# Every fourth unit's input product moves to GpSimd, fed by DMA, and x is fetched batch by batch

## What is computed

```
xp = xn @ w_xproj
dt_in, Bs, Cs = xp[..., :64], xp[..., 64:128], xp[..., 128:]
delta = softplus(dt_in @ w_dt + b_dt)
A = -exp(A_log)                                  # 128 channels x 64 states
h = exp(dt[:, :, None] * A) * h + (dt * xt)[:, :, None] * bt[:, None, :]
y = einsum('bdn,bn->bd', h, ct)                  # at each of 512 tokens
```

## Time and profile before

| | |
|---|---|
| median of 3 runs | 1300.27 us (1299.22 to 1301.88) |
| the profiled execution's own time | 1303.48 us |
| its span, first to last instruction | 1301.3 us |
| DVE busy | 1159.7 us, 89% of the span |
| POOL busy | 810.6 us, 62% |
| ACT busy | 777.0 us, 60% |
| PE busy | 931.7 us, 72% |
| DMA traffic | 155.29 MB, mean 119 GB/s |

### The profile page before, as it was taken

How to read it: one execution, slowest core, us unless ns; L and a number is a source line. 1 busy time by engine, 2 the same in 40 slices (tenths; PEclk the granted TensorE clock), 3 DMA queues, 4 the chain that set the end, 5 groups by cost and what they waited for, 6 DMA issues and landing times. The chain is left out here.

```text
span 1301.3 us, 19507 instructions
## 1 busy us (share of the span) xinstructions
PE 931.7 (72%) x4212; PEld 372.8 (29%) x4212; DVE 1159.7 (89%) x2546; ACT 777.0 (60%) x2103; POOL 810.6 (62%) x509
## 2 busy tenths in 40 slices
PE   4177767786777767777686867767768776867766
PEld 1022222322323222332233322232223322323222
DVE  4389999899898998979899798989999899997993
ACT  3168755586655864657556675457655586555761
POOL 6357766577564765658566675557756576665662
PEclk9559879689796877979778796878878787786977
DMA  4744457342673445534454335734267344663430
GB/s 104 126 113 122 110 123 174 98 130 79 138 171 95 131 110 135 137 91 131 115 136 132 105 98 124 171 101 120 79 144 174 94 133 110 136 157 100 120 98 8
DMA packets 124118, 155.29 MB, mean 119 GB/s; under 512 B 32719, under 2 KB 57056, under 8 KB 124000
## 3 DMA queue, kind: packets, MB, share of 16 engines
q1 hardware_dynamic: 123488, 153.73, 46.4%
q0 software_dynamic: 512, 0.27, 0.3%
HBM read 137.62 MB, written 4.52 MB: 109 GB/s over the span
## 5 line engine op out<-in xcount | busy, mean ns | idle before, releaser
L1381 POOL TENSOR_TENSOR prod<-hst,C 128x1024 f32<-128x1024 f32 x256 | 603.8, 2359 | 436.6 <-DVE hst L1177 431.1
L1177 DVE TENSOR_TENSOR_SCAN hst<-bank,dbx 128x512 f32<-128x512 f32 x512 | 617.5, 1207 | 8.6 <-ACT bank L645 8.4
L645 ACT ACTIVATE bank<-wide,A_rep 128x512 f32<-128x512 f32 x512 | 351.5, 687 | 407.7 <-DVE hst L1177 332.5
L1171 DVE TENSOR_TENSOR dbx<-bank,B 128x512 f32<-128x512 f32 x512 | 342.5, 669 | 77.6 <-PE bank L877 69.8
L877 PE MATMUL bank<-spread,sel_bc 96*128 96x512 bf16 x512 | 220.3, 445 | 118.2 <-DVE dbx L1171 98.9
L659 ACT ACTIVATE prob<-s_sb,nmax 128x96 f32<-128x96 f32 x512 | 183.8, 360 | 0.0
L911 PE MATMUL bank<-prod,sel_red 128*32 128x512 f32 x1024 | 176.5, 769 | 1.5 <-POOL prod L1381 1.5
L921 PE MATMUL bank<-k,q 128*128 128x384 f32 x256 | 137.7, 626 | 42.4 <-DVE nmax L1190 30.7
L877 PEld LDWEIGHTS bank<-spread,sel_bc 96*128 96x128 bf16 x512 | 54.3, 108 | 289.5 <-DVE dbx L1171 239.8
L928 PE MATMUL bank<-ident,prob 128*96 128x128 f32 x512 | 96.2, 321 | 42.5 <-ACT ao L675 42.5
L1386 POOL TENSOR_TENSOR prob<-prob,pinv 128x384 f32<-128x384 f32 x128 | 110.5, 863 | 10.8 <-DVE pinv L1198 7.9
(11 more groups left out here) (175 smaller groups left out, 949.7 us busy)
## 6 DMA issues: line engine op xcount, KB each, us to landing
wide<-rows SPq DMA_DIRECT2D x512, 256.0 KB, 4.4
vw<-v_tok SPq DMA_DIRECT2D x80, 64.0 KB, 3.3
spread<-parts SPq DMA_DIRECT2D x96, 32.0 KB, 1.9
x_sb<-in_L_attn_x_dram SPq DMA_DIRECT2D x8, 256.0 KB, 4.2
rows<-sp_t SPq DMA_DIRECT2D x8, 256.0 KB, 4.3
out_dram<-outb SPq DMA_DIRECT2D x8, 256.0 KB, 4.1
q<-qn SPq DMA_DIRECT2D x112, 16.0 KB
vw<-v_tok SPq DMA_DIRECT2D x16, 48.0 KB, 3.2
```

Source lines behind the costliest of these rows:

```text
L645: nc.scalar.activation(dtP[s % 2][:, :], steps, ACT.Exp, scale=A_rep[:, g:g + 1]) \
L1171: v.tensor_tensor(dbx[:, s % 3, :], steps, B2[p][:, :], ALU.mult).then_inc(dbx_done, 1)
L1177: v.tensor_tensor_scan(hst[:, s % 4, :], dtP[s % 2][:, :], dbx[:, s % 3, :], 0.0, ALU.mult, ALU.add).then_inc(scan_done, 1)
L1381: g.tensor_tensor(prod[:, 2 * (m % 4):2 * (m % 4) + 2, :], hst[:, 2 * (m % 2):2 * (m % 2) + 2, :], C2[p][:, :].unsqueeze(1).to_broadcast([ ...
```

## The change

The product u*B of every unit with q = 3 (16 of the 64 of a batch) is no longer formed by PE and DVE. The u rows of its channels, 96 to 127, are stored to DRAM (`u_rows`), read back by `widen_u` (two DMAs of 256 KB for two units, 16 DMAs a batch, a ring of 2 slots), and multiplied by B on POOL (`pool_input`, a TENSOR_TENSOR of 128x512 from SBUF into `gbx`), in slots 1, 5, 9, ... behind the pair product of that slot. `spread_parts` issues 9 DMAs where it issued 12.

x is no longer kept whole. SP loads batch B + 1 into `x_ln` at the beginning of body B, and once more batch B into `x_res` at m = 10 for the residual. `ln_stats` moves from slot 0 to 3, `ln_aggr` from 2 to 5, the five root steps from slots 4 to 8 to slots 6 to 10; `ln_apply` stays in slot 11. A wait of ACT for the stored rows before `k` is dropped.

The diff, cut to its core:

```diff
-    "ln_stats": 0, "ln_aggr": 2, "ln_root": 4, "ln_apply": 11, "scale_xn": 12, "softplus_exp": 23, "sum": 26,
+    "ln_stats": 3, "ln_aggr": 5, "ln_root": 6, "ln_apply": 11, "scale_xn": 12, "softplus_exp": 23, "sum": 26,
...
+U_SLOTS = 2
+POOL_Q = 3
+PE_Q = 3
+N_PARTS_DMA = 9
...
-            for b in range(1, NB):
-                x_load(b)
...
+                sp.dma_start(dt_rows[p], dtv[:, :]).then_inc(rows_out, 16)
+                sp.dma_start(u_rows[p], uv[32 * POOL_Q:32 * POOL_Q + 32, :]).then_inc(urows_out, 16)
...
+            def widen_u(B, p, m):
+                wait(sp, gbx_done, B * GROUPS + 2 * (m - U_SLOTS) + 2)
+                if m == 0:
+                    wait(sp, urows_out, (B + 1) * 16)
+                flat = u_rows.rearrange("a d t -> (a d t)")
+                for j in range(2):
+                    row = p * 32 + 4 * m + j
+                    src = bass.AP(flat.tensor, flat.offset + row * L, [[0, 64], [2 * L, 2], [1, L]])
+                    sp.dma_start(uwide[m % U_SLOTS][64 * j:64 * j + 64, :, :], src).then_inc(uwide_in[m % U_SLOTS], 16)
...
             def body(B, p):
+                if not last(B):
+                    wait(sp, ln_step, (B - 1) * N_LN + LN["xa"])
+                    x_load(B + 1, x_ln[1 - p], x_in)
                 for m in range(UNIT_PAIRS):
                     if m + SLOTS < UNIT_PAIRS:
                         widen(B, p, m + SLOTS)
                     elif not last(B):
                         widen(B + 1, 1 - p, m + SLOTS - UNIT_PAIRS)
+                    if m % 4 == 3:
+                        if m // 4 + U_SLOTS < GROUPS // 2:
+                            widen_u(B, p, m // 4 + U_SLOTS)
+                        elif not last(B):
+                            widen_u(B + 1, 1 - p, m // 4 + U_SLOTS - GROUPS // 2)
                     if m == ROWS_AT["store"] and not first(B):
                         store(B - 1, 1 - p)
+                    if m == ROWS_AT["store"]:
+                        x_load(B, x_res, xres_in)
...
+                if q == POOL_Q:
+                    return
...
             def unit_scan(B, s):
                 wait(dve, exp_done, B * UNITS + s + 1)
+                i, q = divmod(s, 4)
+                n = PE_Q * i + q
+                if q == POOL_Q:
+                    wait(dve, gbx_done, B * GROUPS + i + 1)
+                    into = gbx[:, i % 2, :]
+                else:
+                    wait(dve, dbx_done, B * PE_Q * GROUPS + n + 1)
+                    into = dbx[:, n % 3, :]
...
+            def pool_input(B, p, i):
+                if i == 0:
+                    wait(pool, done["p"], job_count("p", B, "B"))
+                if i % 2 == 0:
+                    wait(pool, uwide_in[(i // 2) % U_SLOTS], (B * (GROUPS // 2 // U_SLOTS) + i // 2 // U_SLOTS + 1) * 32)
+                wait(pool, scan_done, B * UNITS + 4 * i - 4)
+                g.tensor_tensor(gbx[:, i % 2, :], uwide[(i // 2) % U_SLOTS][:, i % 2, :], B2[p][:, :], ALU.mult) \
+                    .then_inc(gbx_done, 1)
...
                     if s % 2 == 1:
                         pair_product(B, p, s // 2)
+                    if s % 4 == 1:
+                        if s // 4 + 1 < GROUPS:
+                            pool_input(B, p, s // 4 + 1)
+                        elif not last(B):
+                            pool_input(B + 1, 1 - p, 0)
```

More of the change, by code:

```diff
@@ L113 @@
 SLOTS = 4
+U_SLOTS = 2
+POOL_Q = 3
+PE_Q = 3
 UNIT_PAIRS = UNITS // 2
-VIA_DMA = (0,)
-VIA_PE = tuple(i for i in range(2) if i not in VIA_DMA)
-N_PARTS_DMA = 12 * len(VIA_PE)
+N_PARTS_DMA = 9
 SP = {n: i + 1 for i, n in enumerate(
-    ["abs", "relu", "exp", "sum", "ln", "lost", "log1p", "dt", "u"]
-    + [f"{step}{i}" for step in ("hi", "r", "mid", "lo") for i in VIA_PE])}
+    ["abs", "relu", "exp", "sum", "ln", "lost", "log1p", "dt", "u", "hi", "r", "mid", "lo"])}
 N_SP = len(SP)
-PART_STEPS = [f"{step}{i}" for step in ("r", "lo") for i in VIA_PE]
 CV = {n: i + 1 for i, n in enumerate(["v", "tanh", "cs"])}
@@ L195, in hybrid_block_kernel @@
         bias_row = sb("bias_row", [1, D])
-        x_sb = sb("x_sb", [128, NB, NT, D])
+        x_ln = [sb(f"x_ln{p}", [128, NT, D]) for p in range(2)]
+        x_res = sb("x_res", [128, NT, D])
         st = sb("st", [128, NT, 6])
@@ L216, in hybrid_block_kernel @@
         kn = uv[0:KVH * HD, :]
[L217 to L221, removed]
+        dti, dtv, res = sp_l[0:DTR, :], sp_t, sp_r
+        parts = sb("parts", [D, 3, L], BF16)
+        spread = [sb(f"spread{p}", [96, PE_Q, L], BF16) for p in range(2)]
+        dt_rows = nc.dram_tensor("dt_rows", [2, D, L], F32, kind="Internal").ap()
+        wide = [sb(f"wide{c}", [128, 2, L]) for c in range(SLOTS)]
+        u_rows = nc.dram_tensor("u_rows", [2, 32, L], F32, kind="Internal").ap()
+        uwide = [sb(f"uwide{c}", [128, 2, L]) for c in range(U_SLOTS)]
+        gbx = sb("gbx", [128, 2, L])
         qn = sb("qn", [H * HD, L])
@@ new lines, in widen @@
+            def widen(B, p, m):
+                wait(sp, exp_done, B * UNITS + 2 * (m - SLOTS) + 2)
+                if m == 0:
+                    wait(sp, rows_out, (B + 1) * 16)
+                flat = dt_rows.rearrange("a d t -> (a d t)")
+                for j in range(2):
+                    row = p * D + 64 * (m % 2) + 2 * (m // 2) + j
+                    src = bass.AP(flat.tensor, flat.offset + row * L, [[0, 64], [32 * L, 2], [1, L]])
+                    sp.dma_start(wide[m % SLOTS][64 * j:64 * j + 64, :, :], src).then_inc(wide_in[m % SLOTS], 16)
@@ L475, in spread_parts @@
                 for part, made in enumerate(("hi", "mid", "lo")):
-                    for i in VIA_PE:
-                        wait(sp, sp_step, B * N_SP + SP[f"{made}{i}"])
-                        for c in range(4):
-                            sp.dma_start(spread[i][p][32 * part:32 * part + 32, c, :],
-                                         parts[i][32 * c:32 * c + 32, part, :]).then_inc(parts_in, 16)
+                    wait(sp, sp_step, B * N_SP + SP[made])
+                    for c in range(PE_Q):
+                        sp.dma_start(spread[p][32 * part:32 * part + 32, c, :],
+                                     parts[32 * c:32 * c + 32, part, :]).then_inc(parts_in, 16)
             def keys(B):
@@ L505, in front @@
                     widen(B, p, m)
+                for m in range(U_SLOTS):
+                    widen_u(B, p, m)
                 keys(B)
@@ L1101, in setup_step, with ln_stats @@
                     v.tensor_tensor(W2[:, :], wf_abs[:, :], jobP[:, 0:D], ALU.add).then_inc(init, 1)
-            def ln_stats(B):
-                dve.wait_ge(x_in[0], 16)
-                if not first(B):
-                    dve.wait_ge(x_in[1], 16 * (NB - 1))
+            def ln_stats(B, p):
+                wait(dve, x_in, B * 16 + 16)
                 for t in range(NT):
-                    ins = v.bn_stats(st[:, t, :], xin(B)[:, t, :])
+                    ins = v.bn_stats(st[:, t, :], x_ln[p][:, t, :])
                 ins.then_inc(ln_step, 1)
```

150 lines of the change are left out of this document (54 added, 96 removed).

## The result

The changed kernel took 1365.0 us (median; 1360.4 to 1372.1), the kernel before 1299.7 in the same session: a ratio of 1.051, 95% interval 1.045 to 1.056. It is slower by 65 us, where I had forecast 61. The profiled execution, the slowest of the four (1372.1), has a span of 1370.1 us, 68.8 above that of before.

The account below looks back on a forecast made before the run. DVE, busy 89% of the span, was taken to bound the kernel. Saved products (-73.0 us) and the freed aggregation (-9.5) against late x, roots and other terms summed to +61 us on 1300.3: 1361 us, range 1317 to 1395.

Parts of the forecast that it names:

- x comes late: At `ln_stats`, DVE waits for x behind SP's queue: 11.2 us in bodies 1 to 6 (+67), +8.8 in body 0.
- The roots come late: At `ln_apply`, slot 11, DVE waits 4.9 us for POOL's last root step in each of 7 bodies: +34 us.
- `ve` no longer held: The aggregation's last instruction, moved to slot 5, no longer waits out a POOL pair product: -9.5 us.
- Swallowed savings: At slots 19, 27 and 43, 22 saved products are lost again to waits for POOL or PE: +12.5 us.
- Slots 15 and 16: `pool_input` delays root2 by 0.7 us; DVE loses 0.57 and is held 0.8 longer, 7 x 1.4: +9.8 us.
- The traffic of u: DMA traffic grows by 33.5 MB, about a fifth, all fetched 6 units ahead; no term in the sum.
- The last batch: No wait for x, but SP is 2.7 us late and the exp of unit 8 waits for its DMA: +4.3 us.
- z: The slots 15 and 16 term: `pool_input` delays root2 and DVE is held longer, 1.4 us a body.
- ring: POOL as a pace: its backlog after softplus, with the ring letting it trail two units, 1 us in 7 bodies: +7 us.
- The first two rivals: x is there in time, 1285 us, chance 0.09; only x is late, 1298 us, chance 0.06.
- The third: POOL and DVE hold each other at every `pool_input`, 1395 us; chance 0.15.
- The fourth: The change does what it says, x and roots both in time, nothing late: 1218 us; chance 0.03.

Follow-up runs that it names:

- the x half alone: Changed kernel with the u half taken out (every u spread by PE, products on DVE), x per batch issued by SP: 1347.8 us, 1.038 of the kernel before.
- x alone: Changed kernel without the u half, x per batch issued from ScalarE's queue instead of SP's: 1305.6 us, 1.005 of the kernel before.
- the moved roots: Changed kernel with the five root steps in slots 6 to 8, ahead of the probabilities: 1358.8 us; with the value rows moved too, 1344.7 us.

## Why the prediction was right, and where its terms were off

The medians of the runs put the change together step by step:

| step | us | difference |
|---|---|---|
| before | 1299.7 | |
| x per batch, issued by ScalarE | 1305.6 | +5.9 |
| u half without its transfers, its products cut to 4 columns | 1281.2 | -24.4 |
| with the transfers of u | 1306.4 | +25.2 |
| with the products on POOL in full | 1333.7 | +27.3 |
| x issued by SP (the change) | 1365.0 | +31.3 |

With SP issuing x, the terms did well by halves too: 43 us for the x half alone (measured 48) and so 18 for the u half on top of it (17). With x in time they did not. Without their 76 us for x they give 1285 us, and the kernel with x from ScalarE took 1333.7, of which 18.5 are waits for x that are left.

- **x comes late.** Right in mechanism: +67 forecast, 7.3 to 9.4 us instead of 11.2 in each of bodies 1 to 6 (47.3 us), body 0 5.8 instead of 8.8. The runs with another queue give 31 us for it in the full change and 42 with x alone. The arithmetic of SP's queue held to the issue; what I had left out is that the same late queue first holds up DVE itself: around the start of batch 4, 1.6 us at scan 62 and 1.3 at scan 0 for an exp whose delta broadcast is late, and 1.4 at the product of unit 1 behind the keys. Counted from SP's first q issue, DVE came to the statistics after 29.5 us and not after 25.1, and so waited 7.4 us there and not 12.5.
- **The roots come late.** 3.97 us in each of six bodies instead of 4.9 in seven (body 0 shows none), by the mechanism described; in batch 4 DVE had already stood 0.69 us at scan 10 for a pair product. But taking the wait away gave 6 us at most, since DVE's instructions there grew by nearly as much. "It is the wait of POOL on DVE turned round" was the right sentence; 34 us was too high a price for what the order of the steps decides.
- **`ve` no longer held.** Right: 170 ns in all 8.
- **Swallowed savings.** The term most in error. I had 22 of 128 products swallowed, 12.5 us, at slots 19, 27 and 43. Slots 19 and 43 came out as described: the wait at slot 20 grew from 4.30 to 4.89 us, and scans 40 to 43 gained nothing. But these were few of the places. With POOL's products and the transfers out of the way, the u half gained 24.4 us and not 73 - 12.5 = 60.5. By groups of scans against x alone, scans 4 to 7, 12 to 15, 28 to 31, 44 to 47 and 52 to 55 gained the plain 0.6 each and four other groups 0.8 to 1.3; scans 16 to 19, 36 to 39 and 40 to 43 gained nothing or 0.1, and 0 to 3, 8 to 11, 24 to 27 and 60 to 63 took 0.5 to 1.7 us more, where DVE waits for x, the roots, PE's u and the delta broadcasts. In the last four groups the kernel before idles 1.1 us in scans 0 to 3 and nothing in the others; that DVE came there just late enough is my reading.
- **Slots 15 and 16.** Forecast +1.4 a body; scans 16 to 19 took 1.10 us more in the change where a free saving would have been -0.59: 1.7.
- **The traffic of u.** The step that failed outright: it has no term in the sum, only "all of it is fetched 6 units ahead", and the transfers of u cost 25 us, most of it in scans 0 to 3. I had read that u itself is fetched early enough, and it is (16.8 us of POOL's idle time in total); I had not asked what its 33.5 MB do to the other transfers.
- **The last batch.** It became 4.2 us shorter. Against the 9.1 us of its 16 savings that leaves 4.9 given back, where my terms for it (swallowed, z, ring and the late exp) came to 8.4.

The direction and the two late waits were foreseen; that the sum came within 4 us is luck, because its errors cancel: too much for x and the roots, nothing for the transfers, and too large a saving. The first two rivals fell on the waits (x in time; only x late). The third, POOL and DVE holding each other more, was wrong in size (it wanted 34 us more; the `mprob` scalings grew by 15 us in all) but is what the moved roots ran into. The fourth, the full saving, is refuted even with everything else in its favour.

## What to carry to other kernels

A product taken off the engine that bounds the kernel is worth its time only where nothing else stands just behind it; find the places where the engine arrived just late enough for what it needs, because once it comes earlier they swallow the saving (here two thirds of it). Where a load that was made once becomes a load per batch, the first question is whose queue it stands in and behind how many issues, and the second how many bytes are already under way in front of it. And moving a waited-for step ahead on an engine that shares a port with the waiting one can turn the wait into a longer instruction: look at both columns, idle and busy.

## What was unexpected of the hardware

- The landing time of one 256 KB transfer went with what had been issued before it: 3.9 us behind twelve transfers of 64 KB, 8.5 us directly behind eight of its own size, and 9.0 us from ScalarE's queue while SP's was full (6.9 with fewer transfers). Another engine's queue saved the time of issue, not the time of landing. The Trainium skill says that the queues of several engines lead to the same 16 DMA engines (DMA: Bandwidth & Descriptors, "Issuing engines are not separate DMA queues"); these landing times agree with it.
- Making POOL faster did not make every held DVE instruction short again: with products of 4 columns `mprob` took 1651 ns (1588 before, 1933 with full products, both with x from ScalarE), but the step `sp_t<-sp_t,xn` stayed at 1584 ns, 1064 with x alone. I read this as its length depending on which of POOL's instructions it meets, so on the phase of the two engines and not only on POOL's load; no run varied the phase alone.
